# Attention with row sums taken on ScalarE, and a last batch with buffers of its own

## The reference

```python
q = (layernorm(x) @ Wq)            # 32 heads of 32
k, v = ctx @ Wk, ctx @ Wv          # 8 heads of 32, each used by 4 query heads
probs = softmax(einsum('bhqd,bhkd->bhqk', q, k) * 32 ** -0.5)
x = x + einsum('bhqk,bhkd->bhqd', probs, v) @ Wo
xb = layernorm(x).bfloat16()
qg, sg = dynamic_quant(xb * inv_gate); qu, su = dynamic_quant(xb * inv_up)
inter = clip(silu((qg @ w_gate.T) * sg * s_wgate) * ((qu @ w_up.T) * su * s_wup), -10, 10)
qi, si = dynamic_quant(inter * inv_inter)
x = x + (qi @ w_down.T) * si * s_wdown
```

## Time and profile before

| | us |
|---|---|
| median of 3 runs (lowest, highest) | 737.89 (736.92, 738.33) |
| the profiled execution: its own time | 736.11 |
| its span, first to last instruction | 734.3 |
| PE busy | 674.5 (92%) |
| DVE busy | 480.8 (65%) |
| ACT busy | 285.5 (39%) |
| GpSimd busy | 260.3 (35%) |

### The profile page before, as it was taken

How to read it: one execution, slowest core, us unless ns; L and a number is a source line. 1 busy time by engine, 2 the same in 40 slices (tenths; PEclk the granted TensorE clock), 3 DMA queues, 4 the chain that set the end, 5 groups by cost and what they waited for, 6 DMA issues and landing times.

```text
span 734.3 us, 14234 instructions
## 1 busy us (share of the span) xinstructions
PE 674.5 (92%) x5840; PEld 444.2 (60%) x5840; DVE 480.8 (65%) x772; ACT 285.5 (39%) x449; POOL 260.3 (35%) x207
## 2 busy tenths in 40 slices
PE   4999999999999999999999999999899989897743
PEld 3788988867767576656665656655566444443321
DVE  3664241762675585679676877787485877977763
ACT  5343212553534315253434444351524336243330
POOL 5533310030332224423523435241544436535431
PEclk9999999999999999999999999999999999999977
DMA  9778622787570242251325241334314252213000
GB/s 341 243 258 279 216 87 87 237 239 233 169 237 2 55 155 84 88 183 66 84 68 179 89 124 58 87 112 135 94 59 122 88 151 80 73 59 90 29 29 29
DMA packets 46239, 93.58 MB, mean 127 GB/s; under 512 B 6240, under 2 KB 22624, under 8 KB 46176
## 3 DMA queue, kind: packets, MB, share of 16 engines
q1 hardware_dynamic: 43872, 84.30, 37.5%
q0 software_dynamic: 2304, 8.39, 2.9%
HBM read 70.52 MB, written 22.02 MB: 126 GB/s over the span
## 4 chain that ended last, share of the span: by engine, by line
PE 76%; DVE 10%; DMA 4%; ACT 3%; issue 2%; POOL 2%; SPq 1%; POOLq 0%; DVEq 0%; ACTq 0%
PE bank L767 20%; PE bank L680 18%; PE bank L793 6%; PE bank L642 6%; PE bank L655 5%; PE bank_o L731 4%; PE bank L815 4%; PE bank_s L717 3%; PE bank_d L736 3%; PE bank_s L699 3%; DVE neg_max L2176 2%; DMA k_stack<-k_dram 2%; PE bank L665 2%; PE bank L781 2%; DVE amax L2211 1%
## 5 line engine op out<-in xcount | busy, mean ns | idle before, releaser
L680 PE MATMUL bank<-act_t_hi,wq_hi 128*128 128x256 f16 x512 | 139.7, 273 | 0.0
L680 PE MATMUL bank<-act_t_hi,wq_lo 128*128 128x256 f16 x512 | 139.5, 272 | 0.0
L680 PE MATMUL bank<-act_t_lo,wq_hi 128*128 128x256 f16 x512 | 139.4, 272 | 0.0
L2176 DVE TENSOR_REDUCE neg_max<-bank_s 128x4 f16<-128x512 f32 x128 | 83.6, 684 | 45.6 <-PE bank_s L699 45.0
L1607 ACT ACTIVATE probs<-bank_s 128x512 f32<-128x512 f32 x128 | 73.5, 601 | 54.3 <-PE bank_s L717 47.0
L2793 POOL TENSOR_TENSOR wv_hi<-wv_hi,wv_lo 128x512 f32<-128x512 f32 x28 | 37.4, 1343 | 106.2 <-DMA wv_lo<-r_dram 106.2
L1643 ACT COPY q_t<-bank 128x1024 f16<-128x1024 f16 (+1 forms) x48 | 41.7, 869 | 46.4 <-PE bank L781 28.5
L2787 POOL TENSOR_TENSOR xs<-xb,inv_up 128x1024 f32<-128x1024 bf16 x16 | 38.0, 2378 | 57.2 <-ACT code_g L1664 57.2
L680 PEld LDWEIGHTS bank<-act_t_hi,wq_hi 128*128 128x128 f16 x512 | 49.9, 98 | 11.0 <-issue 1.2
L680 PEld LDWEIGHTS bank<-act_t_lo,wq_hi 128*128 128x128 f16 x512 | 50.1, 98 | 9.9
L680 PEld LDWEIGHTS bank<-act_t_hi,wq_lo 128*128 128x128 f16 x512 | 50.0, 98 | 6.0
(11 more groups left out here) (145 smaller groups left out, 1391.7 us busy)
## 6 DMA issues: line engine op xcount, KB each, us to landing
q_stack<-q_dram SPq DMA_DIRECT2D x48, 256.0 KB, 4.5
inp<-in_x SPq DMA_DIRECT2D x16, 512.0 KB, 5.0
wv_lo<-r_dram SPq DMA_DIRECT2D x56, 128.0 KB, 2.8
x<-in_x SPq DMA_DIRECT2D x11, 512.0 KB, 4.4
out<-x POOLq DMA_DIRECT2D x11, 512.0 KB, 3.0
q_dram<-q_st_hi SPq DMA_DIRECT2D x8, 512.0 KB, 3.3
q_dram<-q_st_lo SPq DMA_DIRECT2D x8, 512.0 KB, 3.9
w_gate<-in_ctx_t SPq DMA_DIRECT2D x6, 512.0 KB, 5.1
```

The source lines that it names most:

```text
L680: ins = nc.tensor.matmul(bank[:, :, jj, :], wq_sb[a][:, 2 * item + jj, kc, :], act_t[m][:, kc, :, :], start=(kc == 0 and (a, m) == PARTS[0 ...
L2176: nc.vector.tensor_reduce(neg_max[:, c:c + REP], bank_s[g % 2][:, :].rearrange("p (j n) -> p j n", j=REP), AX_X, ALU.max, negate=True).the ...
```

## The change

Five things change together.

1. The queries are scaled by 32^-0.5 when they are split, so that `s` gives finished scores. After `max_` has read a group, ACT runs `exp_s`: for each of the four heads one activation of 128x128, from the bank back into the same bank, with minus the row maximum as bias and the sum of each row written to one column of `den`. The exponentials themselves are not used; the second pass computes them again, transposed.
2. `recip` inverts `den`, 128x32, before the second pass. `rt` transposes it on PE, `rt_copy` on ACT puts it in r_sb (32x128), and `save_r` and `fill_r` broadcast it as before. The 16 small matmuls of `pv`, `head_sel` and bank_d are gone; bank_s has three banks.
3. `norm` moves from GpSimd to DVE and multiplies straight out of bank_o; `o_out_` on ACT is gone. `pv` waits for `norm_done` in place of `o_out`.
4. The last batch (`LAST`, r = 15) has buffers of its own in the SBUF space of the query weights (`spare`), its own columns of amax, scale and rscale, the two banks bank1 in place of bank3, and its own semaphores for transposes. Its final add is on DVE, and SP stores it in two halves.
5. The lists of all five engines are in a new order.

```diff
+LAST = NB - 1
 def place3(r, name):
+    if r == LAST:
+        return (W3 + G3 + T3).index(name)
...
-        head_sel = sb("head_sel", [P, 2 * NKV + HD - NKV], F32)
-        r_sb = sb("r_sb", [P, P], F32)
+        den = sb("den", [P, NKV * REP], F32)
+        rden = sb("rden", [P, NKV * REP], F32)
+        r_sb = sb("r_sb", [NKV * REP, P], F32)
-        bank_s = [stack.enter_context(nc.psum_tensor(f"bank_s{i}", [P, 512], F32)) for i in range(2)]
+        bank_s = [stack.enter_context(nc.psum_tensor(f"bank_s{i}", [P, 512], F32)) for i in range(3)]
-        bank_d = stack.enter_context(nc.psum_tensor("bank_d", [P, 512], F32))
...
+        def spare(h, start, n, dt):
+            v = flat(wq_sb[h])[:, start:start + (n if dt in (F16, BF16) else 2 * n)]
+            return v if dt == F16 else v.bitcast(dt)
+        def xs_of(r, u):
+            return spare(("hi", "lo")[u], 0, D, F32) if r == LAST else xs[:, :]
...
             def s(p, b, g):
-                if g < 2:
-                    if needed(8 * r - 1 + g):
-                        pe.wait_ge(exp_done, 8 * r - 1 + g)
+                if g < 3:
+                    if needed(8 * r):
+                        pe.wait_ge(exp_done, 8 * r - (1, 0, 2)[g])
                 else:
-                    if needed(8 * r + g - 1):
-                        pe.wait_ge(max_done, 8 * r + g - 1)
+                    pe.wait_ge(den_done, 8 * r + g - 2)
...
+            def rt(p, b):
+                pe.wait_ge(recip_done, r + 1)
+                pe.wait_ge(mt_out, r + 1)
+                nc.tensor.transpose(bank_s[2][0:NKV * REP, P:2 * P], rden[:, :], ident32[:, :]).then_inc(rt_full, 1)
...
             def pv(p, b, t):
                 if needed(2 * r + t):
-                    pe.wait_ge(o_out, 2 * r + t)
+                    pe.wait_ge(norm_done, 2 * r + t)
                 for g in range(4):
-                for j in range(REP):
-                    c0 = (NKV - (REP * t + j)) % NKV
-                    for g in range(4):
-                        ins = nc.tensor.matmul(bank_d[HD * g:HD * g + HD, b * P:(b + 1) * P], head_sel[:, c0:c0 + HD],
-                                               probs[:, g, j * P:(j + 1) * P], start=(t == 0 and j == 0),
-                                               stop=(t == NT - 1 and j == REP - 1), tile_position=(0, HD * g))
...
+            def exp_s(p, b, g):
+                c = REP * (NT * (g % 4) + g // 4)
+                act.wait_ge(max_done, 8 * r + g + 1)
+                if g == 0 and needed(r):
+                    act.wait_ge(recip_done, r)
+                for j in range(REP):
+                    ins = nc.scalar.activation(bank_s[g % 3][:, j * P:(j + 1) * P], bank_s[g % 3][:, j * P:(j + 1) * P], ACT.Exp,
+                                               bias=neg_max[:, c + j:c + j + 1], accum_out=den[:, c + j:c + j + 1])
+                ins.then_inc(den_done, 1)
...
             def recip(p, b):
-                dve.wait_ge(pv_full, 2 * r + 2)
-                nc.vector.reciprocal(r_sb[:, :], bank_d[:, b * P:(b + 1) * P]).then_inc(recip_done, 1)
+                dve.wait_ge(den_done, 8 * r + 8)
+                nc.vector.reciprocal(rden[:, :], den[:, :]).then_inc(recip_done, 1)
+            def norm(p, b, t):
+                dve.wait_ge(pv_full, 2 * r + t + 1)
+                dve.wait_ge(r_filled, r_filled_by(p, b))
+                nc.vector.tensor_tensor(o_raw(p, t), bank_o[:, :], r_rows(p, t, t + 1), ALU.mult).then_inc(norm_done, 1)
...
+            def fin_last_(n):
+                dve.wait_ge(dn_scaled, 2 * LAST + n + 1)
+                nc.vector.tensor_tensor(x2_of(LAST)[:, cols], x2_of(LAST)[:, cols], gu_of(LAST, n),
+                                        ALU.add).then_inc(fin_last, 1)
```

More of the change, by code:

```diff
@@ new lines, in _ @@
+            tq(1, 1, "g")
+            q(4, 2, 2)
+            s(3, 0, 0)
+            pv(2, 1, 1)
+            s(3, 0, 1)
+            s(3, 0, 2)
+            gu(1, 1, "gate")
+            q(4, 2, 3)
+            s(3, 0, 3)
+            tq(1, 1, "u")
+            s(3, 0, 4)
+            q(4, 3, 0)
+            gu(1, 1, "up")
+            s(3, 0, 5)
+            wo_(2, 1, 0, 0, 2)
+            s(3, 0, 6)
+            wo_(2, 1, 0, 2, 3)
+            s(3, 0, 7)
+            wo_(2, 1, 0, 3, 6)
+            mt(3, 0)
@@ new lines, in _ @@
+            wo_(2, 1, 0, 6, 8)
+            wo_(2, 1, 1, 0, 3)
+            rt(3, 0)
+            wo_(2, 1, 1, 3, 5)
+            st(3, 0, 0)
+            st(3, 0, 1)
+            st(3, 0, 2)
+            wo_(2, 1, 1, 5, 7)
+            st(3, 0, 3)
+            st(3, 0, 4)
+            wo_(2, 1, 1, 7, 8)
+            ti(1, 1)
+            st(3, 0, 5)
+            pv(3, 0, 0)
+            dn(1, 1, 0)
+            st(3, 0, 6)
+            dn(1, 1, 1)
+            st(3, 0, 7)
+            q(4, 3, 1)
@@ new lines, in _ @@
+            s(4, 1, 1)
+            pv(4, 0, 1)
+            xt(6, 0, 0)
+            xt(6, 0, 1)
+            gu(3, 0, "gate")
+            s(4, 1, 2)
+            tq(3, 0, "u")
+            s(4, 1, 3)
+            xt(6, 1, 0)
+            xt(6, 1, 1)
+            s(4, 1, 4)
+            gu(3, 0, "up")
+            wo_(4, 0, 0, 0, 2)
+            s(4, 1, 5)
+            wo_(4, 0, 0, 2, 6)
+            s(4, 1, 6)
+            q(6, 0, 0)
+            s(4, 1, 7)
+            wo_(4, 0, 0, 6, 8)
+            mt(4, 1)
@@ new lines, in _ @@
+            wo_(4, 0, 1, 0, 5)
+            st(4, 1, 0)
+            rt(4, 1)
+            wo_(4, 0, 1, 5, 6)
+            st(4, 1, 1)
+            wo_(4, 0, 1, 6, 8)
+            st(4, 1, 2)
+            st(4, 1, 3)
+            ti(3, 0)
+            q(6, 0, 1)
+            st(4, 1, 4)
+            pv(4, 1, 0)
+            st(4, 1, 5)
+            st(4, 1, 6)
+            dn(3, 0, 0)
+            st(4, 1, 7)
+            q(6, 0, 2)
+            dn(3, 0, 1)
+            q(6, 0, 3)
+            tq(3, 1, "g")
@@ new lines, in _ @@
+            hi(3, "q1")
+            exp_s(2, 0, 0)
+            qt(0, 1, 0)
+            exp_s(2, 0, 1)
+            exp_s(2, 0, 2)
+            o_hi_(1, 1, 0)
+            qt(0, 1, 1)
+            exp_s(2, 0, 3)
+            o_hi_(1, 1, 1)
+            hi(3, "q2")
+            exp_s(2, 0, 4)
+            tanh(0, 1)
+            exp_s(2, 0, 5)
+            exp_s(2, 0, 6)
+            mt_copy(2, 0)
+            exp_s(2, 0, 7)
+            code(1, 0, 0)
+            hi(3, "q3")
+            rt_copy(2, 0)
@@ L1880, in _ @@
             exp(2, 1, 7)
-            code(1, 1, 0)
-            code_i(1, 0)
-            hi(5, "q0")
+            o_hi_(2, 1, 0)
+            qt(1, 0, 2)
+            qt(1, 1, 0)
+            code(1, 1, 1)
+            hi(4, "q1")
+            exp_s(3, 0, 0)
+            exp_s(3, 0, 1)
+            exp_s(3, 0, 2)
+            qt(1, 1, 1)
+            o_hi_(2, 1, 1)
+            exp_s(3, 0, 3)
+            hi(4, "q2")
+            tanh(1, 1)
+            exp_s(3, 0, 4)
+            exp_s(3, 0, 5)
@@ new lines, in _ @@
+            o_hi_(4, 1, 1)
+            exp_s(5, 0, 2)
+            qt(3, 1, 1)
+            exp_s(5, 0, 3)
+            exp_s(5, 0, 4)
+            tanh(3, 1)
+            exp_s(5, 0, 5)
+            exp_s(5, 0, 6)
+            exp_s(5, 0, 7)
+            mt_copy(5, 0)
+            rt_copy(5, 0)
+            hi(6, "q1")
+            exp(5, 0, 0)
+            code(4, 0, 0)
+            code_i(3, 1)
+            exp(5, 0, 1)
+            exp(5, 0, 2)
+            exp(5, 0, 3)
+            qt(3, 1, 2)
@@ L2042, in _ @@
-            code(5, 0, 0)
+            o_hi_(6, 0, 1)
+            qt(5, 0, 1)
+            exp_s(6, 1, 0)
+            tanh(5, 0)
             hi(7, "q3")
-            o_hi_(6, 0, 1)
+            exp_s(6, 1, 1)
+            exp_s(6, 1, 2)
+            exp_s(6, 1, 3)
+            exp_s(6, 1, 4)
+            code(5, 1, 0)
+            exp_s(6, 1, 5)
+            exp_s(6, 1, 6)
             mt_copy(6, 1)
+            exp_s(6, 1, 7)
+            code_i(5, 0)
+            qt(5, 0, 2)
+            rt_copy(6, 1)
@@ L2532, in _ @@
             ln2_stats(2, 1)
+            quant(2, 0, 1)
+            lo(4, "q3")
+            norm(3, 0, 1)
             gscale(2, 0, 0)
-            ln2_apply(2, 1)
+            max_(3, 1, 0)
+            lo(5, "x00")
+            lo(5, "x01")
+            max_(3, 1, 1)
+            max_(3, 1, 2)
+            ln2_apply(2, 1)
+            max_(3, 1, 3)
+            lo(5, "x10")
+            max_(3, 1, 4)
+            gscale(2, 0, 1)
+            max_(3, 1, 5)
+            lo(5, "x11")
+            max_(3, 1, 6)
```

2581 lines of the change are left out of this document (1303 added, 1278 removed).

## The result

The changed kernel takes 693.49 us (median of 4 runs, 692.79 to 696.92) against 737.4 us for the kernel before on the same chip: a ratio of 0.9414, with a 95% interval of 0.9379 to 0.9449. The forecast was 697 us. The profiled execution took 692.98 us, its span 691.1.

The account below looks back on a forecast made before the run. TensorE was taken to bound the kernel up to about 657 us, then one batch's dependent chain. Sum: 639.0 - 14.6 + 4 + 30 + 36 = 694.4 us of span, 697 us as time; range 680 to 720.

Parts of the forecast that it names:

- Small matmuls, 31.7 us less `rt`: TensorE: removing 32 groups of small fp32 matmuls saves 31.7 us, the added transposes cost 3 us; net 28.5 us off.
- Rival D: TensorE: the small matmuls hid waits that now show as idle; some 13 of 28.5 us come back, 710 us; chance 0.05.
- Extra waiting, 4 us (0 to 12): VectorE: 12 us more work, going to about 79% busy late on, adds 4 us of waiting, bounds 0 to 12.
- the forecast's sum of PE's work: TensorE's program added up by start intervals: ahead of the last maxima transpose 600 us before, 585.6 after, 14.6 less.
- ACT, interval 0.30 us, nothing late: ScalarE, first pass: exponentials start 0.30 us apart (bounds 0.19 and 0.54), 9.6 us a batch, and nothing is late.
- shortfall table: ScalarE lateness summed over batches by interval: 1.4 us at 0.347, 14 at 0.40, 28 at 0.44, 77 at 0.54.
- Rival A: ScalarE paces the first pass, bias column and sum making the interval 0.38 to 0.44 us; 714 us; chance 0.18.
- The upper bound: ScalarE: exponential interval at most 0.54 us, from four 128x512 activations in a row taking 2.15 us.
- the forecast's alternative: ScalarE: if the sum output costs another operand's 93 ns, the exponential interval is 0.387 us, as in rival A.
- The broadcast of 1/denominator: From `rt` to the multiply: 6.8 us, against 7.0 to 7.2 of TensorE work in batches 13 to 15; up to 0.6 late.
- From the last maxima transpose to the last `wo_`, 30 us: TensorE, end: from that transpose to the end of the last `wo_` 30 us (28 to 34), before 45.3.
- Tail, 36 us (33 to 42): Behind the last `wo_`: with batch 15's own buffers and banks 36 us (33 to 42) instead of 49.9.

## Why the prediction was right, and where it was not

The 43.2 us (1 - 0.9414, times 737.9) come apart along a chain of kernels, each a part of the change further: own buffers and banks in the old kernel 12.8; from there to the new order with the denominators taken early, the exponentials on ACT and the multiply on DVE, but the small matmuls still there, 11.0 (0.9826 to 0.9677); the small matmuls 19.4. Each of the three is uncertain by some 4 us.

- *Small matmuls, 31.7 us less `rt`*: this is the step that failed. "So up to about 657 us each microsecond of PE work taken away counts nearly in full" holds between batches 6 and 12 (11.0 us of 11.9) and not ahead of and behind them: 19.4 us came of it. In the profile, PE's busy time between the two kernels differs by 26.1 us, and 7 us come back as idle time (span less busy, 45.3 in place of 38.3), 3.9 of it in the first 233 us and 3.6 from there to 600. In front a further part came back through the clock: behind its wait of 1.92 us at 187.17 the changed kernel has a granted clock of 0.71 and 0.50 at 188 to 190 and 190 to 192 us, and the kernel with the small matmuls 1.00. Rival D's mechanism is there at about the size that D had, 12 us of 31.7 against its 13; but it is no property of `pv` as a filler while ACT works, as D thought. It lies at the places where PE waits for something else. In front that is the keys, at batch 1 for certain; behind batch 12 no run tells what it is. The attempt to remove the waits for the keys failed, so what the gain would be without them isn't shown.
- *What made up for it*: the sum counted only 14.6 us of PE work ahead of the last maxima transpose and put what the new order brings into the 30 us behind it. The kernel with the old order and own buffers has 45.3 us between these points (640.11 to 685.4), the one with the new order and all small matmuls 31.5 (646.01 to 677.5). So the order's part was seen at the right place. Which of its parts does it, the earlier denominators, the multiply on DVE or the order of the FFN pieces, no run here tells apart; that stays open.
- *Extra waiting, 4 us (0 to 12)*: right in size, and that is luck. The last maxima transpose came 3.2 us later than the forecast's sum of PE's work has it (627.63 against 639.0 - 14.6), but as the remainder of two larger errors. By the same sum, PE's work ahead of it is 600 us before, 585.6 after and 615.3 with all small matmuls put back (30 `pv` more), so it lags behind that sum by 38.8, 42.0 and 30.7 us. As these profiles have it, the other parts of the change took 8.1 us of waiting out ahead of it, and the removal of the small matmuls put 11.3 back. The sum had neither. Of the waits for the multiply only the 1.5 us at 612.28 lie ahead of it. What 12 us more on DVE would have cost stays open: 22 more cost 6 to 9, each uncertain by 4. In the event DVE's busy time fell by 4.3 us, where +12 was forecast. Multiply and reciprocal came about as costed; what changed is how often other instructions of DVE were held up. One group of the kernel before, and the same one after:

```profile
L2206 DVE TENSOR_SCALAR xb<-kv_st,mv,rstd 128x1024 bf16<-128x1024 f32 x5 | 9.0, 1809 | 1.7 <-PE bank L781 1.7
L2206 DVE TENSOR_SCALAR xb<-kv_st,mv,rstd x5: 806/812/4853, 286.5 to 669.5; 128x1024 bf16<-128x1024 f32 x5
```

```profile
L2430 DVE TENSOR_SCALAR xb<-kv_st,mv,rstd 128x1024 bf16<-128x1024 f32 x5 | 5.0, 994 | 2.1 <-PE bank L842 2.1
L2430 DVE TENSOR_SCALAR xb<-kv_st,mv,rstd x5: 802/812/1737, 256.9 to 638.9; 128x1024 bf16<-128x1024 f32 x5
```

The second line of each has the shortest, the median and the longest in ns: the median is 812 in both, and the means differ by one or two long ones. The longest stands beside four instructions of GpSimd in a row, 669.04 to 673.75, and ends 0.55 us after them:

```profile
669.45 4.85 DVE L2206 TENSOR_SCALAR xb<-kv_st,mv,rstd 128x1024 bf16<-128x1024 f32 x1
671.50 2.25 POOL L2798 TENSOR_TENSOR wk_lo<-wv_hi,wk_hi 128x512 f16<-128x512 f32 x2
```

(the first two are in the earlier trace rows.) With 51 us less work on GpSimd there was less to be held up by.

- *ACT, interval 0.30 us, nothing late*: the interval is 0.34, the consequence as forecast, 0.7 us of waits. The shortfall table held at two further points, 26 us against 22 and 69 against 62, so its edge was real: the sum stood at 0.340 with the first loss forecast at 0.347. Rival A had the right mechanism with too dear an instruction. The upper bound was misread: four exponentials in 2.15 us, the last of them 0.60 long, are 0.52 us from start to start, not 0.54; nothing in the forecast hangs on it. The Trainium skill's estimate ("ScalarE: Activation LUTs", What ACT_TABLE_LOAD costs) was 0.294 without the sum; the run without sums shows 0.255, which is less and decides, and the sum costs 0.085 where the forecast's alternative had 0.093.
- *The broadcast of 1/denominator*: from `rt` at 630.83 to the first multiply at 639.65 it took 8.8 us, not 6.8. PE waited for the multiply there by 1.4 us. The other wait, 1.5 us in batch 14, came at least in part of DVE's queue: a quantisation ahead of the multiply ran until 611.58. So late twice, 2.9 us in all, not three times by up to 0.6.
- *From the last maxima transpose to the last `wo_`, 30 us*: 29.8.
- *Tail, 36 us (33 to 42)*: 33.7, and both kernels that tried the own buffers by themselves confirm the step. In it are 3.2 us that the forecast had not: the clock fell in two waits. Without them it is 30.6, as the kernel with the added matmuls shows, below the forecast's low end of 33: the chain was priced some 2 us too dear, and the clock made up for it.

## What to carry to other kernels

PE work taken out of a dense program pays only where PE is dense: look for the places where it waits for data, and count what is removed ahead of them at little. Compare more than one profile before a loss of a few us is put down to a place: unchanged stretches differed by 3.6 us here. A mean busy share says little about a pipeline with short hand-overs: ACT became the bound at 69%, so compare an engine's work between two dependent steps with the time the order leaves there. A wait of two to four microseconds can cost another one to three behind it through the granted clock, and filling it with matmuls that nobody reads, where the bank and the order allow it, is cheap.
